# A fused token model on one core: GpSimd's weight preparation in later stages, small weight products inside the tokeniser's norms, landmark sums of unscaled rows, 95-token tiles

## The chip, the cores and the metric

The kernel runs on one core of one Trainium2 chip. The metric is the device time of one execution in microseconds (us). The time of before is the median of three runs. One more execution was taken by the hardware profiler; all rows below are of that one. Engines are TensorE (PE in rows, PEld for its weight loads), VectorE (DVE), ScalarE (ACT), GpSimd (POOL) and the queue of DMA issues on SyncE (SP).

## What is computed

Eight images and eight texts of 77 tokens of 64 features go through five parts. In short:

```python
t = layernorm(patches) @ W1 + b1             # 64 patches of 192 values for each image
t = layernorm(t); t = concat([t, t, t])      # 192 tokens, three equal copies
h = silu(layernorm(t @ Wp1 + bp1)) @ Wp2 + bp2
h = concat([h, txt])                         # 269 tokens of 64 features
h = h + nystrom_attention(layernorm(h))      # 8 heads of 32, 128 landmarks: means over 3 tokens,
                                             # 6 iterations of a pseudo-inverse, a 33-tap convolution
h = h + experts(layernorm(h))                # 8 experts, gelu, top 2:  gelu(xn*g @ W1 + (b @ W1 + b1)) @ W2
h = h + gaussian_attention(layernorm(h))     # 8 heads: scores exp(-gamma * |q - k|^2), weights scaled by ln_scale
h = h + gated_mlp(layernorm(h))              # shared MLP and 4 experts, top 2
```

The attention normalises its input a second time inside, so that its input is scaled by one root and the residual by another. Weights are prepared on the chip: the experts' first matrices are multiplied by their norm's gain, the norm's offset times the matrix gives a bias (b @ W1), the value and output matrices of the Gaussian attention are multiplied together per head, and its matrices are split into a rounded high and a low part.

## The kernel before, in words

All parts are one program of five stages with a barrier between them. A stage has one block of instructions for each engine, written out in order; there is no scheduler, and semaphores (`sem("...")`, `wait_ge`) order engines against each other. Only the first three stages are touched.

**The tokeniser** (lines 219 to 513). Features stand in the 128 partitions, for two halves of the batch, and tokens in the columns. SyncE issues all loads in one queue; `MB` takes 2 MB of matrices: the Gaussian attention's query and key (`M_Q`), value (`M_VT`) and output (`M_OT`), and the experts' first matrices (`M_F1`). Each of the three token norms is a chain: a product on TensorE gives the variance (lines 381, 393, 406), ScalarE takes the root (270, 278, 288), VectorE the reciprocal (465, 470, 475) and the multiply (468, 473, 478), then comes the next weight product. Between them TensorE runs filler products of 512 columns on a cleared tile `ZK` (`spin(n)`, line 362), whose results nobody reads.

Behind the silu (291) and the last token product (410) VectorE writes the stream `HU` (480). **The landmark norm** follows: rows of four batch pairs are centred (417), squared (297), and their variances taken in tiles of 71 tokens (`UT`; 422). ScalarE takes two roots of them (300: once normalised, and twice), VectorE one reciprocal of both (487), ScalarE widens each token's value over 64 columns (`AW`, 304), and TensorE spreads it back over the features (431), four tiles for each pair of batch pairs and each root. VectorE multiplies (491), ScalarE scales by a third of the gain (`X3`, 311), VectorE sums threes of tokens into the landmark columns of `XAP` (499 to 505), ScalarE writes the token columns of `XAP` (314). The second spread gives `XL` (508), for the residual. At the end TensorE forms the value-output products (444, 16 matmuls) and the experts' bias products (449, 16 matmuls of one column); ScalarE (318) and GpSimd (352, 354) read the first, VectorE (511, with `FB1`) the second. Every f32 matmul is two passes in the trace.

GpSimd clears pads and `AA`, waits for `MB`, scales query and key (333), multiplies the experts' matrices by the gains into `MF` (337), makes the high and low parts `WH`, `WL` (342, 344), copies the selection matrix `SEL` (346), adds the output bias to the residual (`HX`, 349).

**The landmark stage** (570 to 1166) projects landmarks (`proj`, 735) and tokens (`project`, 579), forms the 91x91 landmark scores (747), sums and exponentials for all 8 batches, then runs a loop (`body(b)`) of 12 steps for each batch: a product on TensorE (676), an update on VectorE (1082, 1088), a scaling on ScalarE (864, `f_sa`) that GpSimd subtracts from (944, `f_td`). A table `FRONT` gives the pieces of the next batch that an engine does in step k, for ScalarE the query, the eight exponentials (807, k = 2), and so on.

**The expert stage** (1369 to 1584): 16 steps of hidden products with `MF`, gelu, outputs with `WI`, gates by `SEL` (copied by VectorE, 1535), weighting (1540); GpSimd sums the experts' outputs (`YS`, `YA`, 1580, 1583) once for each batch pair. Before that it clears `WT`, `XK` and `KA` (1572 to 1575), the latter two for the Gaussian attention.

The filler and the waits at the end of the tokeniser:

```python
def spin(n):
    for _ in range(n):
        nc.tensor.matmul(PS[:, SPIN, :], ZK[:, 0:128], ZK[:, :], start=True, stop=True)
```

## Time and profile before

| | |
|---|---|
| runs, us | 757.77, 2143.39, 755.29; median 757.77 |
| profiled execution | 756.43 us, its span 754.4 us |
| TensorE busy | 683.4 us (91%) |
| VectorE, ScalarE, GpSimd busy | 437.3, 345.5, 237.0 us |
| mean granted TensorE clock | 0.926 |

The span runs from the first to the last instruction; the other 2.0 us lie around it. Busy time of TensorE counts filler products too. The granted clock is a share of 2.4 GHz; TensorE has two levels, 1.2 (0.50) and 2.4 GHz (1.00), and a value between is a mean over a stretch that holds both. Stages lie at 0 to 50.9, 52 to 392, 393 to 506, 507 to 687 and 688 to 754 us. An operation's time lasts to the end of its writes, so that the next one on the engine can start before it.

### The profile page before, as it was taken

The numbers are of one execution on the slowest core, as the hardware profiler recorded it, in microseconds if no ns is written. First come the engines' busy times: TensorE is split into PE (matmuls) and PEld (weight loads), VectorE is DVE, ScalarE is ACT, GpSimd is POOL, SyncE is SP. The second block draws the span as 40 slices with busy tenths as digits, with TensorE's granted clock in tenths as the row PEclk, the third lists the DMA queues.
The fourth block names the chain that finished last, engine by engine and source line by source line (L and its number), as shares of the span: only waits on it lengthen the run. The fifth ranks groups of instructions, "written<-read, shape, count | busy, mean of one in ns | idle before, by whom it ended". The sixth has DMA issues, their size and how long they took to land. (4 is left out here: it accounts for less than half of the span.)

```text
span 754.4 us, 14900 instructions
## 1 busy us (share of the span) xinstructions
PE 683.4 (91%) x6016; PEld 528.6 (70%) x6016; DVE 437.3 (58%) x863; ACT 345.5 (46%) x774; POOL 237.0 (31%) x211
## 2 busy tenths in 40 slices
PE   8689688999999989898979999969999999998896
PEld 4488577888798879798867555547666666657565
DVE  3405848686868585958545333325777777764422
ACT  4425443544535445353326555514555555544531
POOL 6433433434454443534431022103222222201001
PEclk9758779999999999999986999975999999997999
DMA  8100000000000000000000000000000000000000
...
DMA packets 4988, 8.47 MB, mean 11 GB/s; under 512 B 3576, under 2 KB 4088, under 8 KB 4536
## 3 DMA queue, kind: packets, MB, share of 16 engines
...
## 5 line engine op out<-in xcount | busy, mean ns | idle before, releaser
L944 POOL TENSOR_TENSOR STD<-STD,NN 91x492 f32<-91x492 f32 (+1 forms) x96 | 104.0, 1100 | 152.2 <-DVE NN L1082 94.1
L676 PE MATMUL PS<-ST 128*91 128x123 f32 x768 | 91.6, 271 | 6.0 <-DVE ST L1088 5.9
L676 PE MATMUL PS<-NN 128*91 128x123 f32 (+1 forms) x768 | 89.3, 267 | 8.6 <-DVE NN L1082 8.5
L676 PEld LDWEIGHTS PS<-NN 128*91 128x91 f32 x768 | 81.3, 159 | 16.8 <-DVE NN L1082 13.0
L676 PEld LDWEIGHTS PS<-ST 128*91 128x91 f32 x768 | 83.3, 159 | 11.3 <-DVE ST L1088 8.3
L1082 DVE SCALAR_TENSOR_TENSOR NN<-ST,PS 91x492 f32<-91x492 f32 x96 | 62.3, 660 | 49.1 <-PE PS L676 49.1
L1704 PE MATMUL PS<-QR,KA 128*128 128x270 f32 x256 | 72.5, 414 | 0.0
L1818 DVE TENSOR_SCALAR CL<-PS,K 128x270 f32<-128x270 f32 x144 | 65.6, 495 | 9.9 <-PE PS L1704 4.5
L864 ACT ACTIVATE STD<-ST 91x492 f32<-91x492 f32 (+1 forms) x96 | 51.4, 561 | 41.0 <-DVE ST L1088 40.9
L1088 DVE SCALAR_TENSOR_TENSOR ST<-PS,STD 91x492 f32<-91x492 f32 (+1 forms) x96 | 55.3, 598 | 11.7 <-PE PS L676 8.6
L1759 ACT ACTIVATE EX<-CL,NG 128x540 f32<-128x540 f32 x64 | 46.7, 741 | 32.8 <-DVE CL L1818 32.8
L1475 ACT ACTIVATE GE<-PS,FB 128x540 f32<-128x540 f32 x64 | 42.5, 708 | 34.4 <-PE PS L1380 34.2
L1635 POOL TENSOR_TENSOR QR<-QR 64x540 f32<-64x540 f32 x32 | 34.6, 1083 | 68.9 <-ACT QR L1750 68.9
L1704 PEld LDWEIGHTS PS<-QR,KA 128*128 128x128 f32 x256 | 46.5, 196 | 10.9 <-issue 2.9
L1795 DVE COPY KA<-PS 64x288 f32<-64x288 f32 x64 | 29.1, 454 | 20.8 <-PE PS L1645 18.4
L1380 PE MATMUL PS<-XM,MF 64*128 64x270 f32 x256 | 40.1, 431 | 0.2
L1719 PE MATMUL PS<-EX,VM 128*64 128x270 f32 x256 | 36.2, 404 | 0.0
L1400 PE MATMUL PS<-GE,WI 128*64 128x270 f32 x256 | 35.8, 403 | 0.0
L1540 DVE SCALAR_TENSOR_TENSOR YW<-PS,WI,WB 128x540 f32<-128x540 f32 x16 | 12.5, 780 | 37.8 <-PE PS L1400 37.8
L807 ACT ACTIVATE E<-PS,M 91x142 f32<-91x142 f32 x64 | 23.0, 373 | 24.2 <-DVE M L996 24.2
L1380 PEld LDWEIGHTS PS<-XM,MF 64*128 64x128 f32 x256 | 22.7, 194 | 15.7 <-issue 8.2
L1645 PE MATMUL PS<-XK,WH 128*128 128x270 f32 x64 | 26.0, 417 | 8.3 <-POOL XK L1631 4.0
...
## 6 DMA issues: line engine op xcount, KB each, us to landing
...
```

Source lines behind the costliest of these rows:

```text
L676: last = nc.tensor.matmul(PS[0:NL, PINV + q, h % 4 * SW + c0:(h % 4 + 1) * SW], x[:, h, 0:NL], x[:, h, c0:SW], start=True, stop=True)
L864: nc.scalar.mul(SA[:, 4 * q:4 * q + 4, c0:SW], ST[0:NL, b % 2, 4 * q:4 * q + 4, c0:SW], S_D).then_inc(sem("f_sa"), 1)
L944: nc.gpsimd.tensor_tensor(TD[:, 4 * q:4 * q + 4, c0:SW], SA[:, 4 * q:4 * q + 4, c0:SW], NN[0:NL, 4 * q:4 * q + 4, c0:SW], ALU.subtract).th ...
L1082: v.scalar_tensor_tensor(out=NN[0:NL, own, :], in0=ST[0:NL, b % 2, own, :], scalar=N_S, in1=heads4(PS[0:NL, PINV + q, 0:4 * SW]), op0=ALU. ...
L1088: v.scalar_tensor_tensor(out=ST[0:NL, b % 2, own, c0:SW], in0=heads4(PS[0:NL, PINV + q, 0:4 * SW])[:, :, c0:SW], scalar=S_M, in1=TD[:, own ...
L1380: last = nc.tensor.matmul(PS[:, HIDDEN + 2 * (j % 2) + o, 0:NP], MF[half, j * 128:(j + 1) * 128], XM[half, p, :], start=True, stop=True)
L1400: last = nc.tensor.matmul(PS[c * D:(c + 1) * D, OUT + o, 0:NP], WI[:, X_F2 + g * D:X_F2 + (g + 1) * D], GE[:, ring(p, g), o, :], start=k = ...
L1475: nc.scalar.activation(GE[:, ring(p, j), :, :], PS[:, HIDDEN + 2 * (j % 2):HIDDEN + 2 * (j % 2) + 2, 0:NP], ACT.Gelu, bias=FB1[:, j:j + 1] ...
L1704: last = nc.tensor.matmul(PS[:, bank, 0:NP], KA[:, a, u, t * 128:(t + 1) * 128], QR[:, a, u, :], start=True, stop=True)
L1719: last = nc.tensor.matmul(PS[t * D:(t + 1) * D, 7 * o, 0:NP], VM[:, o, t, u * D:(u + 1) * D] if u < H else VR[:, o, t, :], EX[:, slot(i, o ...
L1759: nc.scalar.activation(EX[:, n, :, :], CL[:, n, :, :], ACT.Exp, scale=NG[:, u:u + 1]).then_inc(sem("d_e"), 1)
L1818: v.tensor_scalar(CL[:, slot(i, o, u), t, :], PS[:, bank, 0:NP], K2[:, a, c:c + 1], 0.0, ALU.add, ALU.max).then_inc(sem("d_cl"), 1)
```

## The change

Six edits.

- **Loads.** The 2 MB load is split: the experts' matrices go straight to `MF` (1 MB), the value and output ones to `MV` (64 rows), the bias vectors of the experts separately; query and key go last, to the new `MQ`.
- **GpSimd.** In the tokeniser only the clearing and `HX` stay. Scaling and splitting of query and key move behind the second batch pair's sum of the expert stage, the clearing of `XK` and `KA` behind the first. Multiplying `MF` by the gains and copying `SEL` become ten ScalarE operations in the steps of the first batch's loop (`PREPARED`).
- **TensorE's fillers.** The bias products (`ffn_bias`, from the unscaled `MF`) and the value-output products (`value_out`) take the place of fillers in the token norms. VectorE forms `FB1` ahead of the last token norm's reciprocal. 14 fillers stand at the end of the stage.
- **Tiles.** The landmark norm works in three tiles of 95 tokens (the last overlaps), not four of 71; root and reciprocal are taken one by one; ScalarE widens the first half, VectorE the second.
- **Landmark sums.** VectorE sums the unscaled rows into `PL`, and ScalarE scales the sums into `XAP`.
- **High and low parts of value-output.** ScalarE writes `WH` from PSUM, VectorE `WL`. The table load for the exponentials is made in the tokeniser.

The core of the diff:

```diff
...
-                sp.dma_start(MB[:, :], mat[:, W_Q:W_W]).then_inc(sem("more_mats"), 16)
+                sp.dma_start(MF[:, :], mat[:, W_F1:W_W]).then_inc(sem("ffn_mats"), 16)
+                sp.dma_start(MV[:, :], mat[0:D, W_VT:W_F1]).then_inc(sem("vo_mats"), 16)
+                sp.dma_start(WI[:, 0:X_B1 + 2 * E0], wide[:, 0:X_B1 + 2 * E0]).then_inc(sem("ffn_bias"), 16)
...
+                sp.dma_start(MQ[:, :], mat[:, W_Q:W_VT]).then_inc(sem("qk_mats"), 16)
...
-                    act.wait_ge(sem("a_inv"), 1)
-                    nc.scalar.copy(AW[:, n, :, :], AI[:, n, :].unsqueeze(2).broadcast_to([UT, 16, D])
-                                   ).then_inc(sem("a_wide"), 1)
-                    if n:
...
-                        for c in range(2):
...
+                    act.wait_ge(sem("a_inv"), 2 - n)
+                    nc.scalar.copy(AW[:, n, 0, :, :], AI[:, n, 0, :].unsqueeze(2).broadcast_to([TA, 6, D])
+                                   ).then_inc(sem("a_wide_first"), 1)
+                warm(ACT.Exp, 1)
...
-                act.wait_ge(sem("wvo_mm"), 1)
-                nc.scalar.mul(WVO[:, :, :], PS[:, 3, :].rearrange("p (h o) -> p h o", h=H),
-                              VE[:, V_LS:V_LS + 1]).then_inc(sem("wvo"), 1)
+                    if c == 0:
+                        act.wait_ge(sem("wvo_mm"), 1)
+                        nc.scalar.mul(WH[:, Y_VO:Y_W], PS[:, 3, :], VE[:, V_LS:V_LS + 1]).then_inc(sem("wvo_high"), 1)
+                    act.wait_ge(sem("a_pooled"), c + 1)
+                    nc.scalar.activation(XAP[:, s, one + 1:one + 90], PL[:, s, 1:90], ACT.Identity, scale=V3[:, 0:1],
+                                         bias=VE[:, V_BA:V_BA + 1])
...
-                nc.gpsimd.tensor_scalar(MB[:, M_Q:M_Q + 2 * H * D], MB[:, M_Q:M_Q + 2 * H * D],
-                                        VE[:, V_LS:V_LS + 1], None, ALU.mult).then_inc(sem("wqk"), 1)
...
-                    nc.gpsimd.tensor_tensor(MF[:, o * 128:(o + 4) * 128].rearrange("p (e n) -> p e n", e=2),
-                                            MB[:, M_F1 + o * 128:M_F1 + (o + 4) * 128].rearrange("p (e n) -> p e n", e=2),
-                                            VE[:, V_FG + o // 2:V_FG + o // 2 + 2].unsqueeze(2).broadcast_to([128, 2, EH]),
-                                            ALU.mult)
...
-                nc.gpsimd.tensor_copy(WH[:, 0:Y_VO], MB[:, M_Q:M_Q + Y_VO]).then_inc(sem("w_high"), 1)
...
-                nc.gpsimd.tensor_tensor(WL[:, 0:Y_VO], MB[:, M_Q:M_Q + Y_VO], WH[:, 0:Y_VO], ALU.subtract)
...
-                nc.gpsimd.tensor_copy(SEL[:, :], CO[:, C_SEL:C_SEL + E0 * 128])
...
                 nc.gpsimd.tensor_scalar(HX[:, :, :], HU[:, :, :], VE[:, V_BO:V_BO + 1], None, ALU.add)
...
-                wvo = WVO[:, :, :].rearrange("p h o -> p (h o)")
-                nc.gpsimd.tensor_copy(WH[:, Y_VO:Y_W], wvo).then_inc(sem("w_high"), 1)
...
-                nc.gpsimd.tensor_tensor(WL[:, Y_VO:Y_W], wvo, WH[:, Y_VO:Y_W], ALU.subtract)
...
+                    for j in range(first, end):
+                        last = nc.tensor.matmul(PS[:, 2, j:j + 1], MF[0:D, j * 128:(j + 1) * 128],
+                                                VE[0:D, V_FB + j // 2:V_FB + j // 2 + 1], start=True, stop=True)
...
+                    for h in range(first, end):
+                        for o in range(2):
+                            last = nc.tensor.matmul(PS[o * D:(o + 1) * D, 3, h * D:(h + 1) * D],
+                                                    MV[:, M_VT + h * D:M_VT + (h + 1) * D],
+                                                    MV[:, M_OT + h * D:M_OT + (h + 1) * D], start=True, stop=True)
...
-                for c, g, cols, k in parts:
...
-                        pe.wait_ge(sem("a_sq"), c + 1)
-                    last = nc.tensor.matmul(PS[0:UT, 4, k:k + 2], AQ[:, c, cols], CO[:, C_AVG:C_AVG + 2 * D:D],
...
-                spin(2)
...
-                    for c, g, cols, k in parts:
...
-                pe.wait_ge(sem("a_wide"), 1)
-                spread(1, 5)
+                for c in range(2):
+                    spin(1)
+                    pe.wait_ge(sem("a_sq"), c + 1)
+                    for g, cols in enumerate(spans):
+                        k = 6 * c + 2 * g
+                        last = nc.tensor.matmul(PS[0:TA, 4, k:k + 2], AQ[:, c, cols], CO[:, C_AVG:C_AVG + 2 * D:D],
...
+                value_out(7, H).then_inc(sem("wvo_mm"), 1)
+                spin(4)
...
+                    for g, cols in enumerate(spans):
+                        last = nc.tensor.matmul(PS[:, bank, cols], AW[:, n, c, 2 * g:2 * g + 2, :].rearrange("p a d -> p (a d)"),
...
+                pe.wait_ge(sem("a_wide_first"), 1)
+                spread(1, 0, 5)
+                pe.wait_ge(sem("a_wide_second"), 1)
+                spread(1, 1, 6)
...
-                pe.wait_ge(sem("a_wide"), 2)
-                spread(0, 1)
-                pe.wait_ge(sem("more_mats"), 16)
-                for h in range(H):
-                    for o in range(2):
-                        last = nc.tensor.matmul(PS[o * D:(o + 1) * D, 3, h * D:(h + 1) * D],
-                                                MB[0:D, M_VT + h * D:M_VT + (h + 1) * D],
...
-                for j in range(2 * E0):
-                    last = nc.tensor.matmul(PS[:, 0, j:j + 1], MB[0:D, M_F1 + j * 128:M_F1 + (j + 1) * 128],
...
+                pe.wait_ge(sem("a_wide_first"), 2)
+                spread(0, 0, 1)
+                pe.wait_ge(sem("a_wide_second"), 2)
+                spread(0, 1, 2)
+                spin(14)
...
+                dve.wait_ge(sem("fb1_mm"), 1)
+                dve.wait_ge(sem("ffn_bias"), 16)
+                v.tensor_tensor(FB1[:, :], PS[:, 2, 0:2 * E0], WI[:, X_B1:X_B1 + 2 * E0], ALU.add).then_inc(sem("fb1"), 1)
...
-                dve.wait_ge(sem("a_std"), 2)
-                v.reciprocal(AI[:, :, :], AI[:, :, :]).then_inc(sem("a_inv"), 1)
+                for n in (1, 0):
+                    dve.wait_ge(sem("a_std"), 2 - n)
+                    v.reciprocal(AI[:, n, :, :], AI[:, n, :, :]).then_inc(sem("a_inv"), 1)
+                    dve.wait_ge(sem("a_inv"), 2 - n)
+                    v.tensor_copy(AW[:, n, 1, :, :], AI[:, n, 1, :].unsqueeze(2).broadcast_to([TA, 6, D])
+                                  ).then_inc(sem("a_wide_second"), 1)
...
-                for c in range(2):
...
-                    dve.wait_ge(sem("a_third"), c + 1)
...
+                    dve.wait_ge(sem("a_norm"), c + 1)
+                    v.tensor_reduce(PL[:, s, 0:1], a2[:, :, 0:2], AX.X, ALU.add)
...
-                    v.tensor_tensor(XAP[:, s, one + 21:one + 22], XAP[:, s, one + 21:one + 22], X3[:, s, 0:1], ALU.add)
...
-                dve.wait_ge(sem("fb1_mm"), 1)
-                dve.wait_ge(sem("wides"), 16)
-                v.tensor_tensor(FB1[:, :], PS[:, 0, 0:2 * E0], WI[:, X_B1:X_B1 + 2 * E0], ALU.add)
+                dve.wait_ge(sem("wvo_high"), 1)
+                v.scalar_tensor_tensor(out=WL[:, Y_VO:Y_W], in0=PS[:, 3, :], scalar=VE[:, V_LS:V_LS + 1], in1=WH[:, Y_VO:Y_W],
+                                       op0=ALU.mult, op1=ALU.subtract)
...
+                PREPARED = {1: (0,), 3: (1, 8), 4: (2,), 5: (3, 9), 7: (4,), 9: (5,), 10: (6,), 11: (7,)}
+                def prepared(e):
+                    if e < E0:
+                        own = slice(e * EH, (e + 1) * EH)
+                        nc.scalar.mul(MF[:, own], MF[:, own], VE[:, V_FG + e:V_FG + e + 1])
+                    else:
+                        half = (e - E0) * E0 * D
+                        nc.scalar.copy(SEL[:, half:half + E0 * D], CO[:, C_SEL + half:C_SEL + half + E0 * D])
...
+                            for piece in PREPARED.get(k, ()) if b == 0 else ():
+                                prepared(piece)
...
-                for k, (rows, value) in enumerate(((XK[:, :].bitcast(F32), 0.0), (KA[D:128, :, :, :], 0.25))):
...
-                    nc.gpsimd.memset(rows, value).then_inc(sem("clear"), 1)
...
+                    if p == 0:
+                        nc.gpsimd.memset(XK[:, :].bitcast(F32), 0.0).then_inc(sem("clear"), 1)
...
+                        nc.gpsimd.memset(KA[D:128, :, :, :], 0.25).then_inc(sem("clear"), 1)
...
+                    if p == 1:
+                        nc.gpsimd.tensor_scalar(MQ[:, :], MQ[:, :], VE[:, V_LS:V_LS + 1], None, ALU.mult).then_inc(sem("wqk"), 1)
...
+                        nc.gpsimd.tensor_copy(WH[:, 0:Y_VO], MQ[:, :]).then_inc(sem("wqk"), 1)
...
+                        nc.gpsimd.tensor_tensor(WL[:, 0:Y_VO], MQ[:, :], WH[:, 0:Y_VO], ALU.subtract).then_inc(sem("wqk"), 1)
...
```

TensorE, from the last token norm to the first products of the landmark stage; before (`ZK` is a filler, `MB` 64x64 the value-output product, `VE,MB` the bias product, `AW` the spread):

```order
L406 MATMUL PS<-TQ,CO 128x256
L362 MATMUL PS<-ZK 128x512 x10
L410 MATMUL PS<-TC,MA 64x256 x2
L362 MATMUL PS<-ZK 128x512
L417 MATMUL PS<-HU,CO 128x284 x2
L422 MATMUL PS<-CO,AQ 71x2 x8
L362 MATMUL PS<-ZK 128x512 x2
L431 MATMUL PS<-CO,AW 128x71 x16
L444 MATMUL PS<-MB 64x64 x16
L449 MATMUL PS<-VE,MB 128x1 x16
```

and the same place after the change, up to the stage's end (`VE,MF` is the bias product, `MV` the value-output product):

```order
L415 MATMUL PS<-TQ,CO 128x256
L359 MATMUL PS<-VE,MF 128x1 x6
L367 MATMUL PS<-MV 64x64 x12
L354 MATMUL PS<-ZK 128x512
L422 MATMUL PS<-TC,MA 64x256 x2
...
L367 MATMUL PS<-MV 64x64 x2
L354 MATMUL PS<-ZK 128x512 x4
L446 MATMUL PS<-CO,AW 128x95 x12
L354 MATMUL PS<-ZK 128x512 x14
```

The two groups at the end moved up into the place of the ten fillers and those around them, and fillers stand at the end.

ScalarE in the first batch's loop, before (`QM` is the query, `E,Z` the exponentials, `STD` the scaling of one step, two operations):

```order
L800 ACTIVATE QM<-PS 128x476
L864 ACTIVATE STD<-ST 91x492 x2
L807 ACTIVATE E,Z<-PS,M 91x142 x8
L864 ACTIVATE STD<-ST 91x492 x4
L813 ACTIVATE E_<-E_ 71x1456
```

and after:

```order
L812 ACTIVATE QM<-PS 128x476
L858 ACTIVATE MF<-MF,VE 128x256
L886 ACTIVATE STD<-ST 91x492 x2
L819 ACTIVATE E,Z<-PS,M 91x142 x8
L858 ACTIVATE MF<-MF,VE 128x256
L861 CAST SEL<-CO 128x512
L886 ACTIVATE STD<-ST 91x492 x2
L858 ACTIVATE MF<-MF,VE 128x256 x2
L861 CAST SEL<-CO 128x512
L886 ACTIVATE STD<-ST 91x492 x2
L825 ACTIVATE E_<-E_ 71x1456
```

Two of the new operations stand between the exponentials and the next scaling.

GpSimd in the expert stage, before (`YS` and `YA` are the sums of a batch pair):

```order
L1572 MEMSET WT 128x1080
L1575 MEMSET XK 128x288
L1575 MEMSET KA 64x4608
L1580 TENSOR_TENSOR YS<-YW 128x540 x2
L1583 TENSOR_TENSOR YA<-YS 128x540
L1580 TENSOR_TENSOR YS<-YW 128x540 x2
```

and after the change:

```order
L1595 MEMSET WT 128x1080
L1600 TENSOR_TENSOR YS<-YW 128x540 x2
L1603 TENSOR_TENSOR YA<-YS 128x540
L1605 MEMSET XK 128x288
L1607 MEMSET KA 64x4608
L1600 TENSOR_TENSOR YS<-YW 128x540 x2
L1603 TENSOR_TENSOR YA<-YS 128x540
L1610 TENSOR_SCALAR MQ<-MQ,VE 128x1024
L1612 CAST WH<-MQ 128x1024
L1614 TENSOR_TENSOR WL<-MQ,WH 128x1024
L1600 TENSOR_TENSOR YS<-YW 128x540 x2
```

The two clearings went behind the first pair's sum, and the three operations on `MQ` came from the tokeniser.

## Rows read from the trace of the kernel before

**Rows 1.** Windows by stage: us; busy of PE, PEld, DVE, ACT, POOL; clock; DMA.

```profile
0.00:50.90 50.90, 40.99 (x210) 30.36 (x210) 15.87 (x32) 19.84 (x41) 22.98 (x21) 0.78 0.37 137
52.00:62.80 10.80, 9.56 (x48) 8.52 (x49) 1.45 (x2) 4.99 (x15) 4.46 (x6) 0.50 0.01 2
104.00:144.00 40.00, 33.32 (x351) 30.34 (x350) 29.19 (x49) 16.02 (x41) 18.06 (x14) 1.00 0.01 2
```

**Rows 2.** Timeline, the tokeniser's end and the next start: start us, us, engine line operation [idle].

```profile
41.75 1.97 PE L444 MATMUL PS<-MB 64*64 64x64 f32 x32
43.66 6.98 PE L449 MATMUL PS<-VE,MB 64*128 64x1 f32 x32
51.98 1.99 PE L735 MATMUL PS<-XAP,MA 128*128 128x96 f32 x8 [1.34 <-PEq L127]
```

**Rows 3.** Timeline, the landmark norm.

```profile
27.11 1.98 PE L417 MATMUL PS<-HU,CO 128*128 128x284 f32 x4
31.15 1.04 ACT L304 COPY AW<-AI 71x1024 f32<-71x1024 f32 x1 [0.41 <-DVE AI L487]
32.25 3.69 PE L431 MATMUL PS<-CO,AW 71*128 71x71 f32 x16 [1.41 <-ACT AW L304]
34.34 0.45 DVE L491 TENSOR_TENSOR A<-AC,PS 128x284 f32<-128x284 f32 x1 [3.22 <-PE PS L431]
```

**Rows 4.** Windows of 2 us in the tokeniser.

```profile
24.00:26.00 2.00, 0.59 (x4) 0.29 (x4) 0.72 (x1) 1.23 (x2) 1.62 (x2) 0.82 0.00 0
32.00:34.00 2.00, 1.75 (x8) 1.75 (x9) 0.00 (x0) 0.20 (x1) 0.00 (x0) 0.53 0.00 0
46.00:48.00 2.00, 2.00 (x11) 2.00 (x11) 0.00 (x0) 0.00 (x0) 0.49 (x1) 0.50 0.00 0
```

**Rows 5.** Timeline, the last token norm.

```profile
19.81 2.66 PE L362 MATMUL PS<-ZK 128*128 128x512 f32 x10
20.71 1.75 DVE L475 RECIPROCAL TR<-TR 128x256 f32<-128x256 f32 x1 [2.58 <-ACT TR L288]
20.97 1.04 POOL L342 CAST WH<-MB 128x1024 fp32r<-128x1024 f32 x1
22.09 2.35 POOL L344 TENSOR_TENSOR WL<-MB,WH 128x1024 fp32r<-128x1024 f32 x1
22.49 2.23 DVE L478 TENSOR_TENSOR TN<-TB,TR 128x256 f32<-128x256 f32 x1
24.76 0.60 ACT L291 ACTIVATE TC<-TN,VE 128x256 f32<-128x256 f32 x1 [2.57 <-DVE TN L478]
```

**Rows 6.** Timeline, products of the landmark stage's start, at either clock.

```profile
59.94 3.22 PE L579 MATMUL PS<-XAP,MA 128*128 128x238 f32 x8
64.60 1.13 PE L735 MATMUL PS<-XAP,MA 128*128 128x96 f32 x8
```

**Rows 7.** Timeline, the first batch's loop.

```profile
123.35 1.13 ACT L864 ACTIVATE STD<-ST 91x492 f32<-91x492 f32 x2
124.05 2.41 POOL L944 TENSOR_TENSOR STD<-STD,NN 91x492 f32<-91x492 f32 x2 [3.26 <-ACT STD L864]
125.33 1.15 DVE L1024 SCALAR_TENSOR_TENSOR Z<-E,Z 91x8 f32<-91x8 f32 x1
127.12 1.93 PE L676 MATMUL PS<-ST 128*91 128x123 f32 x16 [1.46 <-DVE ST L1088]
```

**Rows 8.** Timeline, GpSimd's moved operations, and VectorE beside its sum in the expert stage.

```profile
13.98 2.85 POOL L333 TENSOR_SCALAR MB<-MB,VE 128x1024 f32<-128x1024 f32 x1 [5.33 <-DMA MB<-mat]
394.67 3.93 POOL L1575 MEMSET KA<- 64x4608 f32 x1
426.43 1.34 POOL L1580 TENSOR_TENSOR YS<-YW 128x540 f32<-128x540 f32 x1 [27.83 <-DVE YW L1540]
427.04 0.72 DVE L1535 COPY WB<-PS 128x540 f32<-128x540 f32 x1 [0.76 <-PE PS L1389]
446.03 1.34 POOL L1580 TENSOR_TENSOR YS<-YW 128x540 f32<-128x540 f32 x1 [7.28 <-DVE YW L1540]
```

109 lines of the change are left out of this document (56 added, 53 removed).

## The prediction

> **What bounds the kernel now.** I read the windows by stage first, then the timeline of the first stage from its end backwards, then the stages that the moved work goes to.
>
> The first stage, the tokeniser, takes 50.9 us of the 754.4 us span, with TensorE busy 41.0 us at a mean granted clock of 0.78 [rows 1]. Busy says little here: much of it is filler. What the reader is to see is the stage's end [rows 2]. The last 32 passes of the value-output product (1.97 us) and the 32 passes of the expert bias product (6.98 us) run alone, after everything else, up to 50.64; VectorE then adds the bias vector, which ends the stage at about 50.8, and the next stage's first product starts at 51.98. Ahead of them lies the landmark norm, a chain through all engines [rows 3]: centre at 27.11, widening of the reciprocal roots on ScalarE (1.04 us for 1024 columns), spreading from 32.25 at 3.69/16 = 0.23 us a pass, first product on VectorE at 34.34. The clock explains its pace [rows 4]: 0.82 in 24 to 26, where TensorE waits for the silu and is busy 0.59 us of 2, then 0.53 in 32 to 34, and 0.50 in 46 to 48, although TensorE is busy all of those 2 us, with one-column products. So one-column products did not bring 2.4 GHz back. The next stage then opens at 1.2 GHz for 10.8 us [rows 1].
>
> The token norms ahead [rows 5] are a chain ScalarE, VectorE, TensorE too. GpSimd's subtraction (22.09 to 24.44) lies over the last multiply, which takes 2.23 us where a VectorE product of more columns takes 0.45 alone [rows 3].
>
> **The change part by part.** All sums are against the profiled execution: 756.43 us, span 754.4 and 2.0 around it; the median of the three runs is 757.77. A measurement of this kernel tells about 2% from no change.
>
> Step 1, GpSimd out of the tokeniser: of its operations in the tokeniser [rows 5, 8] only the residual's bias addition and the clearing stay. The last multiply should take about 0.45 us, like the 128x284 product of [rows 3]: 1.8 us less; I put the one of the norm before at 0.2 less, an estimate. The transfer of the expert matrices is 1 MB instead of 2, and is needed at about 15, where GpSimd had the 2 MB at 13.98 [rows 8], so I add no wait.
>
> Step 2, the bias products as filler. Six of them (12 passes) stand between the variance product and the value-output ones, and VectorE's bias addition waits for them **ahead of the last reciprocal** in its queue; behind that reciprocal wait the multiply, the silu and all that follows. A pass took 6.98/32 = 0.218 us at 1.2 GHz [rows 2]. At 2.4 GHz the trace has none; bounds are the smaller pass of the value-output product, 0.062, and 0.218. I scale by the projection, 8 passes in 1.99 us at the low clock and 1.13 at the high one [rows 2, 6], a ratio of 0.57, so 0.124. What follows the variance product started at 19.81 [rows 5], now at 19.6; the 12 passes end at 21.1, the addition (about 0.2) at 21.3, the reciprocal (1.75) at 23.05, the multiply at 23.55. The silu starts at 23.6 instead of 24.76: 1.2 us earlier, where 2.0 were to be had. At 1.2 GHz the passes take 2.6 us and the variance product 0.3 more: the silu starts at 25.1, 0.3 later than before.
>
> Which clock? Before, filler products of 512 columns, three and three, stood between 15 and 18; now 10 one-column products stand there, and the end of the stage shows such products running for 7 us without the clock's coming back [rows 2, 4]. I take it that the clock falls somewhere between 17 and 22 and is back by the landmark norm, whose products are as they were. The Trainium skill, page "TensorE: Matmul & The Clock Gate", Part 1, says that the clock is released by TensorE's being busy and taken back when it idles. Read plainly, that rule lets the bias products hold 2.4 GHz, and the sum would be that of the first rival.
>
> Step 3, from the centred rows to the spreads (27.11 to 32.25, 5.1 us). The second root no longer holds the first reciprocal (about 0.2); 384 columns are widened on each of two engines instead of 1024 on one (1.04 x 384/1024, with a fixed part about 0.5: 0.5 less); 6 variance passes instead of 8, a shorter reciprocal (0.3). 1.0 us less. Spreads start at 32.25 + 0.3 - 1.0 = 31.55.
>
> Step 4, the rest of the stage. Four spreads of 6 passes, 24 x 0.23 x 0.57 = 3.15 us at 2.4 GHz (5.5 at 1.2), then 14 filler products, at 2.66/10 each with the tail counted once, 3.3 us (up to 6 at 1.2). TensorE ends at 31.55 + 6.45 = 38.0. VectorE needs six passes (0.8), then twice a product and its sums (0.45 + 1.0), two products (0.9) and the value-output's low part (0.7): 5.3 us, under TensorE's 6.45; ScalarE's table load now lies in its wait for the first product. The value-output and bias products are gone from the end. The stage ends at 38.0 instead of 50.8: **12.8 us less**. With the clock low to the end, the norm's passes and the four fillers ahead put the spreads at about 33.3; 5.5 + 6 behind that is 44.8: 6.0 less.
>
> Step 5, the next stage. In 52 to 62.8 TensorE is busy 9.56 us at 0.50 [rows 1]; one projection takes 3.22 us [rows 6]. At 2.4 GHz 43% of 9.56 would go, 4.1 us; with the clock lost again at the stage's start nothing. Each later group is paced by VectorE and ScalarE, so it isn't given back. The filler ends just ahead of this stage; I take **3.0 us less**.
>
> Step 6, ten ScalarE pieces in the first batch's loop, eight of 128x256 and two of 128x512. Bounds of the first: above 0.35, below the silu's 0.60 [rows 5]; I take 0.45, and 0.65 for the others, 4.9 us in all. Nine lie in stretches where ScalarE waits. Two of the ten (1.1 us) stand straight behind the eight exponentials and ahead of the scaling that starts at 123.35; GpSimd's subtraction waited for that one (124.05), and VectorE's update (ended by 127.1) for it [rows 7]. But VectorE was also held there, by a tiny operation of 91x8 that took 1.15 us beside GpSimd's, and which now runs before it. I count **0.5 us more**, between 0 and 1.1; 4.9 if nothing is hidden.
>
> Step 7, GpSimd in the expert stage. Clearing KA (3.93 us [rows 8]) moves from 394.67 into GpSimd's idle 7.28 us ahead of the sum at 446.03. The scaling (2.85), cast (1.04) and subtraction (2.35) make 6.2 us [rows 5, 8] and go into the next gap, which is as long (the pattern repeats for each pair): hidden by 1.0 us. VectorE reads PSUM and at most one SBUF operand there; its copy of 540 columns out of PSUM took 0.72 us right through GpSimd's sum of 426.43 to 427.77 [rows 8]. Nothing. The Trainium skill, page "SBUF — State Buffer", section "Who interferes with whom", warns that a VectorE instruction with two SBUF inputs contends with GpSimd's reads, and one with a single input does not; by it too nothing is added here, and step 1 gains.
>
> Sum: -12.8 - 3.0 + 0.5 = -15.3, so 756.4 - 15.3 = **741.1 us**.
>
> **Rivals.**
> - *The clock never falls.* Step 2 gains 1.2; the token product and centring run at 2.4 GHz (0.5 and 0.65 less); spreads start at 32.25 - 1.2 - 1.15 - 1.0 = 28.9, the stage ends at 35.35 (15.5 less), and the next gains 4.1: 756.4 - 15.5 - 4.1 + 0.5 = 737.3. For it: five more products and longer ones in the norm. Against it: [rows 4].
> - *The clock is low to the stage's end.* The stage gains 6.0, and the fillers at the end warm the next, 3.5: 756.4 - 9.0 = 747.4. For it: spreads alone did not raise it in 32 to 42.
> - *The moved work isn't hidden.* ScalarE's 4.9 in place of 0.5 and GpSimd's 6.2 in the expert stage: 741.1 + 4.4 + up to 6.2 = 746 to 752. Against it: step 7's gaps.
> - *Slower: the low clock in the attention loop.* The loop's steps take 1.93 us of 16 passes each, at clock 1.00 [rows 1, 7]. If the change left TensorE at 1.2 GHz there, a step would take 1.93/0.57 = 3.4, 1.5 us more, and each of the eight batches has 12 steps. Eleven steps eat the gain; one batch costs 17.6 us and ends at 759. Against it: the clock was 1.00 over the whole first batch, and nothing in the loop's TensorE work changes.
>
> **How the numbers follow.** Forecast 0.49, clock never falls 0.27, low to the end 0.15, not hidden 0.06, slower 0.03. The forecast's own range is 738 to 744 (steps 5 and 6 at their ends). The range 735 to 748 leaves out part of the last two and the tail of the first. Two per cent under 757.77 is 742.6: all of the second case but little of the third lies below it, and seven tenths of the first, so faster 0.62, same 0.35, slower 0.03.
>
> **What would show it.** Right: the stage's last filler ends near 38; VectorE's bias addition is the operation that the last reciprocal waits behind, and ends after the root; the last multiply takes under 0.7 us; the clock has a low stretch that starts between 17 and 22; the first projection takes near 1.1 us; in the first batch the scaling behind the exponentials starts 1.1 us later after them. Wrong: GpSimd's sums of the expert stage starting late, VectorE copies there over 0.8 us, a stage end past 42, or a clock below 1 in the first batch.

## The result, and the profile after

The changed kernel took 749.02 us (median of four, 745.92 to 750.07) against 758.88 us for the kernel before (median of four, one of them 2143.39; 757.77 without it): ratio 0.9878, 95% interval 0.9848 to 0.9909. Here and below, ratios leave out executions more than 1.5% above the fastest of their kernel, and medians in us keep them. Forecast were 741.1 us and a range of 735 to 748, so the gain came out at some 9 us where 15.3 was expected, and the time lies just above the range. The chance of a gain over 2% was put at 0.62; it was 1.2%. The execution profiled took 745.92 us, span 743.9.

First the windows of the changed kernel, cut where the granted clock (PEclk) changes and at the stage's end; [rows 1, 4] are their counterparts.

```profile
core 0: us, PE busy (x) PEld busy (x) DVE busy (x) ACT busy (x) POOL busy (x), PEclk, DMA share, GB/s
0.00:18.60 18.60, 17.10 (x89) 10.70 (x89) 6.10 (x9) 8.74 (x22) 7.82 (x10) 1.00 0.88 277
18.60:42.50 23.90, 22.07 (x105) 18.14 (x104) 9.04 (x27) 11.94 (x24) 1.71 (x1) 0.50 0.16 66
42.50:44.70 2.20, 2.20 (x10) 1.46 (x8) 0.00 (x0) 0.00 (x0) 0.00 (x0) 1.00 0.00 0
45.80:66.40 20.60, 17.41 (x207) 15.10 (x208) 11.42 (x27) 11.09 (x46) 11.60 (x12) 1.00 0.01 2
```

The clock falls at 18.6, inside the interval the forecast named, and stays at 1.2 GHz until 42.5: through the silu, the landmark norm and the spreads. TensorE is busy in 22.07 of those 23.9 us. The forecast had the clock back by the norm. The stage's last filler ends at 44.7, not 38.0.

The timeline of the same stage (start, duration, engine, line, operation; in brackets idle time and what ended it), for [rows 2, 3, 5, 6]:

```profile
15.23 1.94 PE L359 MATMUL PS<-VE,MF 64*128 64x1 f32 x16
17.63 0.43 DVE L481 TENSOR_TENSOR TN<-TB,TR 128x256 f32<-128x256 f32 x1
20.61 2.72 PE L359 MATMUL PS<-VE,MF 64*128 64x1 f32 x12
20.71 0.47 ACT L295 ACTIVATE TR<-PS,CO 128x256 f32<-128x256 f32 x1 [0.95 <-PE PS L415]
23.36 0.17 DVE L484 TENSOR_TENSOR FB<-PS,WI 128x16 f32<-128x16 f32 x1 [5.30 <-PE PS L359]
23.45 1.74 DVE L486 RECIPROCAL TR<-TR 128x256 f32<-128x256 f32 x1
25.23 0.42 DVE L489 TENSOR_TENSOR TN<-TB,TR 128x256 f32<-128x256 f32 x1
25.69 0.60 ACT L298 ACTIVATE TC<-TN,VE 128x256 f32<-128x256 f32 x1 [2.99 <-DVE TN L489]
...
35.19 5.27 PE L446 MATMUL PS<-CO,AW 95*128 95x95 f32 x24
...
40.16 4.54 PE L354 MATMUL PS<-ZK 128*128 128x512 f32 x14
...
45.85 1.10 PE L747 MATMUL PS<-XAP,MA 128*128 128x96 f32 x8 [1.14 <-PEq L127]
```

A bias pass takes 1.94/16 = 0.12 us at 2.4 GHz and 2.72/12 = 0.23 at 1.2. The root is ready at 21.2, but the reciprocal starts at 23.45: it stands in VectorE's queue behind the bias addition, which waits for the slow passes. The spreads take 0.22 us a pass.

The next stage did gain. Its first product runs at 2.4 GHz, and from the first product to the last of its eight maxima of scores it took 32.8 us (45.85 to 78.7) against 37.3 (51.98 to 89.3). These are the maxima of the kernel before and of the changed one (the last times in a row are the first and the last start):

```profile
L1103 DVE TENSOR_REDUCE MX<-PS x8: 904/914/915, 58.3 to 89.3; 91x8 f32<-91x728 f32 x8
```

```profile
L1126 DVE TENSOR_REDUCE MX<-PS x8: 904/912/915, 50.0 to 78.7; 91x8 f32<-91x728 f32 x8
```

Two later differences don't last. The first batch's loop took 42.2 us instead of 38.8 (97.4 to 139.6 against 107.7 to 146.5), with the clock at 1.2 GHz from 100.5 to 107.3; and the way from the last batch's first update to the first expert row took 57.2 us instead of 60.3. The experiments show that both are where the clock's steps happened to fall in this execution. They also come as a pair: of the nineteen profiles beside this one, two more (mix and late_fill_again below) have a first batch of 42.2 us with the clock low from about 99, and both have 57.3 us on the way to the experts; those with 39.3 us have 59.0 to 61.8. What ties the two is not shown.

### The profile page after: what moved, and what is told of

Same layout as the page of the kernel before. It is cut to its first block and busy times, and to the rows that moved or that the text cites. A ratio compares the mean times of both kernels' runs of the same rounds, so it can differ in the third digit from the quotient of the medians.

```text
span 743.9 us, 14894 instructions
## 1 busy us (share of the span) xinstructions
PE 679.5 (91%) x6006; PEld 524.8 (71%) x6006; DVE 435.1 (58%) x867; ACT 349.2 (47%) x787; POOL 229.6 (31%) x204
## 5 line engine op out<-in xcount | busy, mean ns | idle before, releaser
L688 PEld LDWEIGHTS PS<-NN 128*91 128x91 f32 x768 | 82.1, 160 | 17.2 <-DVE NN L1105 13.2
L1105 DVE SCALAR_TENSOR_TENSOR NN<-ST,PS 91x492 f32<-91x492 f32 x96 | 62.3, 660 | 49.1 <-PE PS L688 49.1
L886 ACT ACTIVATE STD<-ST 91x492 f32<-91x492 f32 (+1 forms) x96 | 51.6, 564 | 40.2 <-DVE ST L1111 40.2
L1791 ACT ACTIVATE EX<-CL,NG 128x540 f32<-128x540 f32 x64 | 46.8, 743 | 32.8 <-DVE CL L1850 32.7
L1498 ACT ACTIVATE GE<-PS,FB 128x540 f32<-128x540 f32 x64 | 42.2, 708 | 34.6 <-PE PS L1403 34.6
L1827 DVE COPY KA<-PS 64x288 f32<-64x288 f32 x64 | 29.1, 454 | 20.4 <-PE PS L1677 17.9
L1403 PE MATMUL PS<-XM,MF 64*128 64x270 f32 x256 | 39.7, 430 | 0.4 <-ACT GE L1498 0.4
L1563 DVE SCALAR_TENSOR_TENSOR YW<-PS,WI,WB 128x540 f32<-128x540 f32 x16 | 12.5, 780 | 37.9 <-PE PS L1423 37.9
```

Of the source, the lines that this page charges most:

```text
L688: last = nc.tensor.matmul(PS[0:NL, PINV + q, h % 4 * SW + c0:(h % 4 + 1) * SW], x[:, h, 0:NL], x[:, h, c0:SW], start=True, stop=True)
L886: nc.scalar.mul(SA[:, 4 * q:4 * q + 4, c0:SW], ST[0:NL, b % 2, 4 * q:4 * q + 4, c0:SW], S_D).then_inc(sem("f_sa"), 1)
L1105: v.scalar_tensor_tensor(out=NN[0:NL, own, :], in0=ST[0:NL, b % 2, own, :], scalar=N_S, in1=heads4(PS[0:NL, PINV + q, 0:4 * SW]), op0=ALU. ...
L1403: last = nc.tensor.matmul(PS[:, HIDDEN + 2 * (j % 2) + o, 0:NP], MF[half, j * 128:(j + 1) * 128], XM[half, p, :], start=True, stop=True)
L1498: nc.scalar.activation(GE[:, ring(p, j), :, :], PS[:, HIDDEN + 2 * (j % 2):HIDDEN + 2 * (j % 2) + 2, 0:NP], ACT.Gelu, bias=FB1[:, j:j + 1] ...
L1791: nc.scalar.activation(EX[:, n, :, :], CL[:, n, :, :], ACT.Exp, scale=NG[:, u:u + 1]).then_inc(sem("d_e"), 1)
```

## The experiments

Medians are given with that of the kernel before on the same chip in the same rounds; fb1_late, no_end_spin, no_pieces and fillers_back share one set of it (758.28), and so do after_again, undo_bias, mix and pool_back (756.69). Single executions of one kernel scatter here over up to 16 us and go with TensorE's mean clock (the changed kernel: 738.01 us at 0.946, 754.22 at 0.922), so medians of six tell some 3 us, and I lean on the traces for less.

**VectorE's queue: fb1_late.** The bias addition moves behind the last multiply.

```diff
-dve.wait_ge(sem("fb1_mm"), 1); dve.wait_ge(sem("ffn_bias"), 16); v.tensor_tensor(FB1...)
 ... reciprocal, multiply (tp_done) ...
+dve.wait_ge(sem("fb1_mm"), 1); dve.wait_ge(sem("ffn_bias"), 16); v.tensor_tensor(FB1...)
```

> The changed kernel with VectorE's bias addition (FB1) moved from ahead of the last reciprocal of the tokeniser to behind the last multiply; nothing else. In the changed kernel TensorE's clock fell at 18.6 us and stayed low to 42.5, the addition waited for the bias products until 23.36, and the silu came at 25.69 (forecast: 23.6). Theory A (the products that took the fillers' place stream too few columns, the clock falls whatever VectorE does): the clock still falls at about 18.6 and is low to about 42, but the silu comes 2.2 us earlier, at 23.5, and the next stage's first product at 43.5 to 44.5 in place of 45.85: total 1.5 to 2 us below the changed kernel's 745.9. Theory B (the wait of VectorE's queue made the long gap, and the gap the low clock): the clock is back within some us after 23.5, the next stage opens at 38 to 39.5, total 739.

747.57 us (before 758.28), ratio 0.9863 (0.9829 to 0.9896); once more, beside pool_back_again: 746.57 (0.9806, 0.9745 to 0.9868). The clock is low from 21.1 to 41.6 all the same, so theory A holds over B on what lowers it. On the gain it was too high: the silu comes at 23.96, 1.7 us earlier, but only 0.6 reach the next stage (45.2, where 43.5 to 44.5 were expected), and the timeline shows why:

```profile
21.10 2.72 PE L359 MATMUL PS<-VE,MF 64*128 64x1 f32 x12
23.75 1.55 PE L367 MATMUL PS<-MV 64*64 64x64 f32 x24
23.96 0.60 ACT L298 ACTIVATE TC<-TN,VE 128x256 f32<-128x256 f32 x1 [0.77 <-DVE TN L486]
25.23 0.79 PE L354 MATMUL PS<-ZK 128*128 128x512 f32 x1
25.95 0.69 PE L422 MATMUL PS<-TC,MA 64*64 64x256 f32 x2
```

The silu ends at 24.56, but the token product starts at 25.95: the moved products and a filler, slow at 1.2 GHz, still stand in front of it. In mix (below) it starts at 24.60.

**The end fillers: no_end_spin.** The changed kernel without its last `spin(14)`.

> The changed kernel without the fourteen fillers behind the last spread. They ended at 44.7 us, VectorE's last work of the stage at 41.6. Theory E (they lengthen the stage and give nothing back): the next stage's first product comes at 42.7 in place of 45.85, and all of the 3.1 us is kept, total 742.8. Rival (they bring the clock back and the next stage is paid for with it): the first product comes at 42.7 but at 1.2 GHz, the scores of the next stage take as long as in the kernel before (its stage lost 4.3 us against the changed kernel's), total 745.9 to 747.

748.88 us, ratio 0.9875 (0.9841 to 0.9909). The rival holds: the next stage opens 3.0 us earlier (42.8), the clock stays at 1.2 GHz from 19.0 to 53.1, and the maxima run from 49.1 to 79.9 instead of 50.0 to 78.7. The fillers pay for themselves; no more.

```profile
L1125 DVE TENSOR_REDUCE MX<-PS x8: 904/912/915, 49.1 to 79.9; 91x8 f32<-91x728 f32 x8
```

**ScalarE's pieces: no_pieces.** They are not issued in the loop. SEL is copied by GpSimd, and the scaling of MF by the gains is left out, so this kernel leaves out a part of the computation.

> The changed kernel without ScalarE's ten pieces in the first batch's loop: the scaling of MF by the gains is left out, and SEL is copied by GpSimd behind HX. The first batch's loop took 42.2 us there and 38.8 before. Theory P (the pieces delay ScalarE's scaling in the loop): it falls to 38.8 to 39.2, total 742.5. Theory C (the loop's start fell into a stretch at 1.2 GHz, 100.5 to 107.3 us, and the pieces cost what was forecast, 0.5): it falls to 41.5 to 41.9, the whole difference sits at the first four steps and is still there, total 745.4.

747.25 us, ratio 0.9872 (0.9831 to 0.9913). The first batch takes 38.8 us, as theory P has it, but fb1_late and no_end_spin, with the pieces, took 39.3, so the pieces cost 0.5 us, and what is left of the 42.2 isn't theirs: theory C has the price right. A piece of MF took 0.51 us, one of SEL 0.64.

**The same kernel again: after_again.**

> The changed kernel once more, word for word. In its first profile the start of the first batch's loop met a stretch at 1.2 GHz (first batch 42.2 us; 39.1 to 39.3 in three kernels with the same loop), and the way from the last batch's first update to the first expert row took 57.2 us (60.4 to 61.7 in four kernels with the same code there). Theory L (where the clock steps down and up differs from execution to execution of one program, and both were accidents of that execution): this profile shows the first batch at 39 to 39.5 and the way to the experts at 60 to 62, its own time is 747 to 750, the median 747.5 to 750. Rival (both belong to the kernel): 42.2 and 57.2 again.

751.66 us (before 756.69). Its ratio, 0.980, rests on two of six executions and isn't used. Theory L holds for the two stretches: first batch 39.3, way to the experts 61.8. Its times were missed: the profiled execution took 754.22 us and the median is above 750. Here the clock is low from 13.1 to 16.5 and from 19.9 to 47.2. A third set (after_third) gave 747.42 against 755.10, ratio 0.9898 (0.9856 to 0.9941), with 39.3 and 59.0 and a low clock from 19.0 to 42.9. The sixteen executions have a median of 749.1.

**The moved products: undo_bias and mix.** In undo_bias the norms' waits hold 512-column fillers alone again, and both groups of products stand behind the spreads; mix keeps what it can of the change. In both VectorE's bias addition is also last in its queue; fb1_late has shown that this alone doesn't hold the clock.

```diff
 # mix, TensorE
-ffn_bias(0, 8)
+spin(3); ffn_bias(0, 4)
-ffn_bias(8, 10)
+spin(3)
-ffn_bias(10, 2 * E0); value_out(0, 6); spin(1)
+spin(10)
 ... the silu's product, then value_out in the later waits ...
-spin(14)
+ffn_bias(4, 2 * E0); spin(4)
```

> The changed kernel with its second part undone: the waits hold 512-column fillers alone, as before (3, 3, 10, 1, 1, 1, 2), and the value-output and bias products stand behind the spreads, in place of the 14 fillers there, with VectorE's addition last. Theory A (the products that took the fillers' place let the clock fall at 18.6): the clock is high to the silu as in the kernel before (to 25.3 there), the silu comes at 23.0 to 23.7, the spreads start at 31 to 32, the products behind them add 4.0 us at 2.4 GHz or 8 at 1.2: first product of the next stage at 41.5 if the clock holds, 46 if not; total 742 to 749. Rival (the fall has nothing to do with them): low from 18 to 21 on here too, silu at 23.5 at the earliest, first product at 46 or later, total 749 or more.

> The changed kernel with before's fillers (3, 3 and 10) in the waits of the two norms, four of sixteen groups of bias products in the first, the value-output products in the waits behind the silu with three fillers, no filler ahead of the centring and none between the two centred halves, and the other twelve groups of bias products and four fillers behind the spreads. Theory A: high clock to the silu (23.4) and from about 29 on; the spreads start at 31.5 to 32.5, last 3.2 to 3.6 us, the products behind them 3 to 3.6 us; first product of the next stage at 39 to 41; total 741 to 744, median some 4 us below the changed kernel's. Rival (before's fillers keep the clock only to the silu, and what follows is too thin whatever stands there): low from 25 to 42, the spreads 5.3 us, first product at 45 to 46, total as the changed kernel.

undo_bias 748.54 us, ratio 0.9883 (0.9848 to 0.9919); mix 747.09, 0.9868 (0.9833 to 0.9904). Windows of mix (columns as above), and from its timeline the spreads, the bias products and the next stage's first product:

```profile
0.00:25.00 25.00, 21.75 (x101) 13.09 (x102) 8.28 (x11) 12.73 (x29) 7.82 (x10) 1.00 0.85 269
25.00:30.00 5.00, 4.94 (x53) 3.53 (x50) 2.38 (x7) 3.08 (x8) 1.71 (x1) 1.00 0.00 0
30.00:35.00 5.00, 5.00 (x43) 4.86 (x43) 4.05 (x18) 4.83 (x11) 0.00 (x0) 0.96 0.00 0
35.00:40.00 5.00, 3.88 (x13) 2.98 (x14) 0.43 (x2) 0.00 (x0) 0.41 (x1) 0.50 0.00 0
```

```profile
30.05 2.81 PE L447 MATMUL PS<-CO,AW 95*128 95x95 f32 x24
...
32.79 3.69 PE L359 MATMUL PS<-VE,MF 64*128 64x1 f32 x24
...
39.60 2.00 PE L749 MATMUL PS<-XAP,MA 128*128 128x96 f32 x8 [1.12 <-PEq L127]
```

The clock holds to 34.6, where it is lost under 24 one-column passes; the spreads take 2.81 us; the next stage opens at 39.6 (undo_bias: 40.1, clock low from 13.2 to 16.7 and again from 37.1). So the fillers that the change took out did keep the clock for this stage. But the next one now opens at 1.2 GHz, stays so to 51.6, and has its last maximum at 77.5: of the 6.3 us won at its start, 1.2 are left, and the median is 2 us below the changed kernel's, not the 4 expected.

```profile
L1128 DVE TENSOR_REDUCE MX<-PS x8: 906/915/916, 45.9 to 77.5; 91x8 f32<-91x728 f32 x8
```

One profile each would be thin proof, since the clock's steps move. All twenty together say it more exactly. In the nine with the change's own products behind the last variance (the changed kernel three times, fb1_late and pool_back twice each, no_end_spin, no_pieces) the clock fell at 18.6 to 21.1 and stayed low to 41.3 or later (after_again was low from 13.1 to 16.5 as well). In the ten with ten fillers there (before, before_warm, undo_bias, mix, mix2, mix3, no_bias, late_bias, late_fill twice) it fell at that place in three, at 19.3 to 20.4, and was back by 23.8 at the latest. fillers_back, with seven fillers among the products, lies between: low from 20.5 to 34.1. So the swap's price is less the fall than the missing return. One-column and 64-column products were swapped together; no run tells their shares apart.

**More fillers: fillers_back, mix2, mix3, before_warm.** fillers_back has 7 fillers among eight groups behind the tp variance; mix2 and mix3 are mix with 2 and 4 fillers ahead of each four of the last twelve groups and at the end; before_warm is the kernel before with 6 fillers ahead of the spreads, 8 between them, and 2 ahead of each four bias groups.

> The changed kernel with 512-column fillers back in the waits of the norms: 3 ahead of the first three groups of bias products, 3 in the next wait, 7 among eight groups behind the tp variance, one or two ahead of and behind the value-output products, which all stand behind the silu now; the last five groups of bias products run behind the spreads, with VectorE's addition last (they lie in bank 0 as in the kernel before). Theory A (too few columns): the clock stays at 2.4 GHz from the start to the silu and over most of the landmark norm, the silu comes at 23.4 to 24.4, the spreads take 3.1 to 3.5 us in place of 5.27, the next stage's first product comes at 38 to 40 in place of 45.85; total 739 to 741 against 745.9. Rival (the clock falls for another reason, such as the total of work up to then): low from about 18 to 25 on all the same, spreads 5.3 us, first product at 43.5 or later, total 744 or more.

> The kernel mix with the twelve groups of bias products behind the spreads broken up: two 512-column fillers ahead of each four groups and two behind them, in place of four fillers at the very end. In mix the next stage's first product came at 39.6 us, as the forecast had it, but the clock had fallen at 34.6 under the bias products and the next stage was run at 1.2 GHz to 51.6: its first maximum of scores came 6.3 us after the first product (4.1 in the changed kernel) and its last at 77.5 (78.7). Theory A (columns streamed while the bias products run keep the clock up into the next stage): no fall between 25 and 45, first product at 39.0 to 40.0, first maximum at 43.5, last at 72.5 to 74.5; total 738 to 742, median 4 to 6 us below the changed kernel's. Rival (the stretch at 1.2 GHz comes all the same, since the next stage opens thin): it only moves to 45 or later, last maximum at 77 or later, total 744 or more.

> As mix2, with four fillers at each of the four places instead of two: 8 more fillers, 2.0 us more at 2.4 GHz (0.25 each). Theory A: if two at a place are enough, this is 2.0 us worse than mix2 (first product at 41 to 42); if two are too few and four are enough, last maximum at 74.5 to 76 and total 740 to 744. Rival: no clock is won, first product at 43 or later, total 748.

> The kernel before, with more 512-column fillers and nothing else: 6 in place of 2 ahead of the first spreads, 8 between the two sets of spreads, and 2 ahead of every four of the last 16 groups of bias products. Theory C (most of what this stage has to give is TensorE's clock, 1.2 GHz from 32.1 to 62.8 there): the spreads take 2.2 us a set in place of 3.7, the products behind them 5 in place of 9, the next stage opens at 46 to 47 in place of 52.0 and runs 3 to 4 us faster: total 747 to 750 against 756.4, as much as the whole change gives. Rival (the change's gain is its own: GpSimd gone, the products out of the end, fewer passes): the fillers lengthen the stage as much as the clock shortens it, first product at 50 to 53, total 754 to 758.

fillers_back 747.50 us (0.9862, 0.9832 to 0.9893), mix2 748.50 (before 756.85; 0.9864, 0.9811 to 0.9917), mix3 752.58 (0.9911, 0.9872 to 0.9950), before_warm 756.78 (0.9994, 0.9964 to 1.0024). None of the gains expected came, and in each case the rival was nearer. That of before_warm matters most: more fillers alone give the kernel before nothing, so what the change gains is its own. In fillers_back the clock was low from 20.5 to 34.1, and the fillers, now slower (three take 1.65 us, 0.96 at 2.4 GHz), held the token product to 28.2 with the silu done at 24.5. In mix2 it fell at 30.2 (after a first low stretch from 20.0 to 23.4), and the timeline of before_warm shows best which work goes with the low clock:

```profile
31.49 2.00 PE L431 MATMUL PS<-CO,AW 71*128 71x71 f32 x16 [0.48 <-ACT AW L304]
33.30 2.09 PE L362 MATMUL PS<-ZK 128*128 128x512 f32 x8
35.72 1.98 PE L431 MATMUL PS<-CO,AW 71*128 71x71 f32 x16 [0.34 <-ACT AW L304]
...
40.77 1.22 PE L362 MATMUL PS<-ZK 128*128 128x512 f32 x2
41.92 1.86 PE L452 MATMUL PS<-VE,MB 64*128 64x1 f32 x8
```

Eight fillers in a row between the spreads keep a set at 2.0 us (3.7 before). Two between bias groups don't: low from 39.8 to 60.3, and TensorE runs 3 us of such work a group of eight passes and two fillers. The products at the end start 4.1 us earlier than before (37.63 against 41.75), the next stage only 1.0.

**GpSimd's work: pool_back.** fb1_late, with the MQ chain of the expert stage back in the tokeniser, its subtraction three times over, and MQ's transfer one place earlier in the queue.

> The kernel of the first set in which VectorE's addition stands behind the last multiply, and besides with GpSimd's work on MQ (scale, round, and the subtraction three times over, some 11 us) back in the tokeniser, with MQ's transfer one place earlier; it no longer stands in the expert stage. Theory G (GpSimd beside VectorE is what made the last multiply take 2.23 us; it takes 0.43 without): the multiply into TN ahead of the silu takes 1.8 to 2.3 us again, the silu comes 1.5 to 2 us later (25.5 to 26 in place of 23.96), and the total grows by up to 2 us. Rival (the long multiply came from the transfers still landing then, which have moved too): it stays at 0.43 us and the silu at 24.

> pool_back once more. Theory E (GpSimd's chain on MQ costs time in the expert stage, which pool_back doesn't have): median 741 to 744 again, and at least 3 us below fb1_late_again. Rival (it was hidden there, and three of six executions met a lucky place of the clock's steps): median 745 to 749, within 2 us of fb1_late_again; with the first six, single times from 740 to 752.

742.76 and 748.55 us (ratios 0.9814, 0.9767 to 0.9861, and 0.9874, 0.9828 to 0.9921), twelve executions together 746.7; fb1_late's twelve 747.5, so in the time the rival of pool_back_again holds. The rows are VectorE's, of fb1_late and of pool_back:

```profile
23.50 0.42 DVE L486 TENSOR_TENSOR TN<-TB,TR 128x256 f32<-128x256 f32 x1
```

```profile
23.23 1.71 DVE L494 TENSOR_TENSOR TN<-TB,TR 128x256 f32<-128x256 f32 x1
```

With GpSimd's subtraction beside it (19.88 to 27.16) the multiply takes 1.71 us (1.40 in pool_back_again), and the silu comes 1.0 later (24.98), where 1.5 to 2 were expected. In the expert stage nothing is to be seen of the chain: the 16 rows YW span 73.7 us with it and without it.

**The products left out, and put elsewhere: no_bias, late_bias, late_fill.** no_bias is mix without the bias products (FB1 is a copy of the expert biases), so it leaves that part of the computation out; two fillers stand in their place in the first wait and ten behind the spreads. late_bias computes them again, in the next stage's waits; late_fill adds fillers where that stage opens:

```diff
+# next stage, ahead of each of the last six projections (bank 4, free columns)
+for g in BIAS.get(2 * p + part, ()):
+    nc.tensor.matmul(PS[:, PROJ, 4 * KP + g:4 * KP + g + 1], MF[0:D, g * 128:(g + 1) * 128], ...)
+# late_fill: 512 columns of WH into bank 7
 proj(0, 0)
+wide(4)
 proj(0, 1)
+wide(4)
```

> The kernel mix with the 32 passes of the bias products left out (FB1 is a copy of the expert biases alone), two fillers in the place of those in the first wait and ten behind the spreads. Theory A (the thin bias products are what brought the clock down ahead of the next stage): high clock from 5 to beyond 45 us, first product of the next stage at 36.3 to 38.0, first maximum of scores 4.1 us later, last at 69.5 to 71.5 (78.7 in the changed kernel, 77.5 in mix); total 736 to 740. Rival (the next stage opens so thin that its clock falls whatever stands ahead of it): first product at 37, but low from 40 or 45 on, first maximum 6.3 us behind the first product, last maximum at 74 to 76; total 741 to 745.

> The whole computation again: no_bias with the 16 groups of bias products put into the next stage, two or three groups ahead of each of the last six projections there (bank 4, columns the projections leave free), and VectorE's addition ahead of that stage's shift. Theory P (the products are harmless where VectorE and ScalarE set the pace and TensorE has wide columns around them): first product of the next stage at 36.3 as in no_bias, last maximum of scores at 71.5 to 73.5 (71.9 there, 78.7 in the changed kernel), total 737 to 743, median within 2 us of no_bias's 740.6 and 6 to 9 us below the changed kernel's. Rival (they cost their 4 to 7 us wherever they stand): last maximum at 76 to 78, total 744 to 748.

> late_bias with four 512-column fillers (of WH's value-output part) after each of the first two projections of the next stage. In no_bias the clock fell there at 37.8 and was back at 44.6, and the first maximum came 5.4 us behind the first product (4.1 at 2.4 GHz). Theory A: the clock holds from 5 to beyond 50 us, the first maximum comes at 40.4 to 41.0, the last at 70.5 to 72.5: 1 us below late_bias. Rival (the fillers stand in front of the scores and the clock falls all the same): first maximum at 42 to 44, total 1 to 3 us above late_bias.

> late_fill once more. If its gain is real (Theory A: no fall of the clock before 60 us): median 742 to 746, first product at 36.0 to 36.3 and the last maximum of scores at 71 to 75. Rival (six lucky executions): median 747 or more.

no_bias 740.55 us (before 758.72), ratio 0.9756 (0.9710 to 0.9803): without the products the forecast's time is there, though not by the forecast's terms (the next stage opens at 36.3, and the clock is low there from 37.8 to 44.6, so theory A was near in the time and wrong on the clock). late_bias 749.03 us (before 757.83), 0.9856 (0.9817 to 0.9894): the rival holds, with the last maximum at 78.4, and the clock low from 20.4 to 23.8, 30.7 to 37.5 and 44.3 to 47.7. late_fill 744.49, 0.9837 (0.9791 to 0.9883), and in the last set 742.85 beside 747.42 of the changed kernel, 0.9824 (0.9789 to 0.9858); its twelve executions have a median of 744.0. It is the best version that computes everything, about 5 us below the changed kernel and 13 below the one before. Windows and products of late_fill's first profile:

```profile
30.00:35.00 5.00, 4.92 (x34) 4.17 (x32) 4.23 (x17) 4.59 (x10) 0.00 (x0) 1.00 0.00 0
35.00:40.00 5.00, 3.87 (x28) 3.26 (x28) 0.00 (x0) 0.97 (x2) 3.65 (x6) 1.00 0.00 2
40.00:45.00 5.00, 5.00 (x48) 4.51 (x47) 1.45 (x2) 2.59 (x11) 0.86 (x1) 1.00 0.02 3
```

```profile
36.13 1.10 PE L752 MATMUL PS<-XAP,MA 128*128 128x96 f32 x8 [1.21 <-PEq L127]
37.01 1.18 PE L741 MATMUL PS<-WH 128*128 128x512 f32 x4
38.03 1.02 PE L752 MATMUL PS<-XAP,MA 128*128 128x96 f32 x8
38.84 1.18 PE L741 MATMUL PS<-WH 128*128 128x512 f32 x4
39.95 0.59 PE L764 MATMUL PS<-STD 32*96 32x96 f32 x16
40.47 0.83 PE L747 MATMUL PS<-VE,MF 64*128 64x1 f32 x6
```

The clock is at 1.00 from 7 to 61.7 us. Maxima of no_bias and of late_fill:

```profile
L1126 DVE TENSOR_REDUCE MX<-PS x8: 904/913/915, 41.7 to 71.9; 91x8 f32<-91x728 f32 x8
```

```profile
L1136 DVE TENSOR_REDUCE MX<-PS x8: 904/914/915, 40.6 to 73.2; 91x8 f32<-91x728 f32 x8
```

The 1.3 us more at the last, after 1.1 less at the first, are the products' price in their new place: 2.4 us by this pair of profiles. In late_bias, with the clock lost twice, it is 4.4 (first maximum 43.8, last 78.4). So it is not nothing, as theory P had it, and between 2.4 and the lower end of the rival's 4 to 7. The margin is thin: in late_bias and in late_fill_again the clock fell at 30.7 and 30.3, under the same spreads as in no_bias, and the stage opened at 39.7 and 39.2 instead of 36.1. The gain of late_fill came again in its second set, theory A's unbroken clock did not.

## Why the prediction was wrong, step by step

**Step 1** was right: both multiplies took 0.42 to 0.43 us, and pool_back brings the long one back.

**Step 2** holds the failure. Its mechanism was right (the addition holds the reciprocal from 21.2 to 23.45, 2.3 us; 0.12 and 0.23 us a pass; the clock falls at 18.6), but from "the clock falls somewhere between 17 and 22 and is back by the landmark norm, whose products are as they were" the second half was wrong. Steps 3 and 4 were summed at 2.4 GHz and ran at 1.2. [Rows 4] had shown the norm at 0.53 in 32 to 34 before the change, and the 0.23 us a pass of [rows 3] was a pass at 1.2 GHz; products "as they were" had thus not kept 2.4 GHz to the spreads. What showed in its place: 1.2 GHz from 18.6 to 42.5, and where wide fillers stand in the waits (mix, undo_bias) 2.4 GHz over the whole norm. The change's own fillers ahead of the spreads ran at 1.2 GHz themselves (0.52 us each in the norm's end) and put the spreads 1.1 us later than their weights were ready. The silu came at 25.69, even past the 25.1 of the low branch.

**Steps 3 and 4.** At 2.4 GHz they are borne out: in mix, centring to spreads takes 4.2 us (25.84 to 30.05; forecast 4.1), the spreads 2.81 (3.15), and the next stage opens at 39.6, where a stage end at 38.0 and the gap of 1.1 give 39.1 (in part luck, since mix has bias products and four fillers there, not fourteen fillers). At 1.2 GHz the low rival had the mechanism: stage end 44.8 forecast, 44.7 measured; 747.4 us forecast. The 0.1 is luck: the spreads started at 35.19 instead of 33.3, and the fillers took 4.5 us instead of 6, since the clock came back under them at 42.5. That was the case to prefer, and I gave it 0.15. Its sign, a stage end past 42, was named in the forecast and came. The difference to the forecast at the stage's end is 6.7 us.

**Step 5** gave 4.5 us, not 3.0: first product to last maximum 32.8 against 37.3. It is not free, though. no_end_spin shows that the gain is what the fillers at the end buy with 3.0 us, and mix that a stage which ends 6 us earlier with its clock lost pays most of it back there. The forecast treated the two stages as terms of a sum; they are tied by the clock that the first hands on. The rival "the clock never falls" (737.3) had the tie in it. That late_fill's profile, with the clock up to 61.7, took 737.5 is chance all the same: its stage ended at 34.9 (35.35 in the rival), but the next took 37.1 us from first product to last maximum, 0.2 less than before and not 4.1, and the first batch (37.9 us) and the way to the experts (57.4) gave 3.8 us that the rival hadn't in it.

**Step 6** was right: 0.5 us, between 38.8 and 39.3 (its nine pieces in waits and two behind the exponentials are one more than the ten there are). The other 2.9 of the first batch's 3.4 are a stretch at 1.2 GHz that two more profiles of the same kernel don't have; so the named sign "a clock below 1 in the first batch" came, but by the execution and not by the change.

**Step 7** was right: nothing. The 16 rows YW of the expert stage span 73.7 us before and after. The rival "the moved work isn't hidden" (746 to 752) covers the measured time all the same, for a cause that these two steps exclude.

The profile's own balance: 6.1 us at the next stage's opening, 4.5 in it, 0.3 lost up to the loop (18.4 to 18.7), 3.4 lost in the first batch, 3.1 won before the experts, 0.5 in all that follows: 10.5, the difference of the spans. Against the medians it is 8 to 10.

What stays open: what decides, from one execution to the next, whether the clock falls under the spreads at 30 us, with the same products ahead of them. And pool_back's first set (three executions at 740) was not repeated; fb1_late_again has two such executions (739.4 and 739.9), so it speaks for the scatter and not for the edit. Each stage time is that of one profile; in the changed kernel's three the next stage opened at 45.85, 49.05 and 46.12.
